# Expert rows loaded transposed, in place of a transpose on TensorE and a copy on VectorE

## What is computed

```python
# layer 1
z = layernorm(x)
agg = (adj > 0) @ z / max(degree, 1)
x = x + relu(concat(z @ W_self + b_self, agg @ W_nb + b_nb) @ W_comb + b_comb)
# layer 2: E = 8 experts, the best 2 of them for each row
xf = layernorm(x)
logits = xf @ Wg + bg
topk_scores, topk_idx = top_k(logits, 2)
topk_w = softmax(topk_scores)
h = gelu(einsum('nd,edh->neh', xf, W1) + b1)       # D = H = 256
y = einsum('neh,ehf->nef', h, W2) + b2
x = x + sum(topk_w * y[the two experts of the row])
```

## Time and profile before

| | |
|---|---|
| median of 3 runs | 551.37 us (549.81 to 551.41) |
| the profiled execution's own time | 551.93 us |
| its span | 550.1 us |
| PE busy | 439.9 us, 80% |
| DVE busy | 391.1 us, 71% |
| ACT busy | 272.6 us, 50% |
| POOL busy | 288.2 us, 52% |
| HBM read and written | 96.52 MB and 26.93 MB |

### The profile page before, as it was taken

The page is one execution under the profiler, slowest core; times in us unless marked ns, Lnnn a source line. Parts: engine busy times, 40 slices in busy tenths (PEclk is TensorE's granted clock), DMA queues, the critical chain, the costliest instruction groups (busy, mean ns, idle before and its releaser), DMA issues.

```text
span 550.1 us, 13137 instructions
## 1 busy us (share of the span) xinstructions
PE 439.9 (80%) x4321; PEld 382.9 (70%) x4321; DVE 391.1 (71%) x1197; ACT 272.6 (50%) x435; POOL 288.2 (52%) x305
## 2 busy tenths in 40 slices
PE   0015999999999999999999999635599999997730
PEld 0014889899898989898988898524378888786520
DVE  5717855686588888878857887574677777679871
ACT  3675452364255353654434444322367777776530
POOL 3993223234156575756564752646545556564570
PEclk9999999999999999999999999955989999999975
DMA  9975999999989999999996944512555555588565
GB/s 248 251 238 119 270 291 298 272 256 269 240 252 250 284 271 308 268 296 271 270 285 184 282 141 139 183 39 98 185 182 163 161 157 156 156 291 342 184 203 153
DMA packets 46785, 122.49 MB, mean 223 GB/s; under 512 B 8953, under 2 KB 18045, under 8 KB 45568
## 3 DMA queue, kind: packets, MB, share of 16 engines
q1 hardware_dynamic: 28896, 68.02, 47.4%
q0 software_dynamic: 16080, 50.49, 28.5%
q10 hardware_dynamic: 1744, 3.15, 2.1%
HBM read 96.52 MB, written 26.93 MB: 224 GB/s over the span
## 4 chain that ended last, share of the span: by engine, by line
PE 33%; DVE 15%; issue 15%; DMA 14%; POOL 13%; ACT 6%; SPq 1%; DVEq 1%; ACTq 1%; another core or an unknown queue 1%; POOLq 0%
PE bank L1224 8%; PE bank L1239 7%; PE bank L1115 5%; PE bank L1116 5%; DMA stage<-in_adj_dram,gidx 5%; POOL dispatched L545 4%; POOL stage L534 4%; DMA wst<-in_L_ffn_W_dram 4%; PE bank L1124 3%; PE bank L1211 2%; DMA stage<-in_adj_dram 2%; POOL z_lo L560 2%; DVE mask L769 2%; DMA x_sb<-in_x_dram 1%; DVE maskT L776 1%
## 5 line engine op out<-in xcount | busy, mean ns | idle before, releaser
L1115 PE MATMUL bank<-z_flat,maskT 128*128 128x257 f16 x1024 | 226.7, 273 | 0.0
L1116 PE MATMUL bank<-z_lo,maskT 128*128 128x256 f16 x1024 | 226.7, 273 | 0.0
L595 POOL DMA_INDIRECT pair_out<-rows,enum x78 | 80.9, 1038 | 64.8 <-DVE gate L1055 34.2
L534 POOL DMA_INDIRECT stage<-in_adj_dram,gidx x64 | 66.2, 1034 | 86.4 <-PE bank L1124 41.6
L1115 PEld LDWEIGHTS bank<-z_flat,maskT 128*128 128x128 fp8e4 x1024 | 100.2, 98 | 12.2
L1116 PEld LDWEIGHTS bank<-z_lo,maskT 128*128 128x128 fp8e4 x1024 | 100.2, 98 | 11.5
L545 POOL DMA_INDIRECT dispatched<-rows,slot x64 | 70.3, 1098 | 26.5 <-issue 19.2
L648 ACT ACTIVATE rows<-bank,rdeg 128x256 f16<-128x256 f32 x32 | 15.1, 473 | 134.3 <-DVE rdeg L829 110.7
L622 ACT ACTIVATE mask<-stage,m 128x2048 fp8e4<-128x2048 int32 x32 | 64.4, 2013 | 20.0 <-DMA stage<-in_adj_dram,gidx 17.9
L1224 PE MATMUL bank<-stage,w 128*128 128x256 f16 x468 | 61.3, 284 | 12.8 <-DVE stage L1028 11.0
L1239 PE MATMUL bank<-w,stage 128*128 x468 | 60.5, 278 | 9.9 <-DVE stage L1042 5.7
(11 more groups left out here) (175 smaller groups left out, 636.5 us busy)
## 6 DMA issues: line engine op xcount, KB each, us to landing
stage<-in_adj_dram SPq DMA_DIRECT2D x128, 256.0 KB
stage<-dispatched SPq DMA_DIRECT2D x39, 260.0 KB
wst<-in_L_ffn_W_dram SPq DMA_DIRECT2D x16, 256.0 KB
z_lo<-pair_out SPq DMA_DIRECT2D x4, 1024.0 KB
maskT<-pair_out SPq DMA_DIRECT2D x4, 1024.0 KB
out_dram<-x_sb SPq DMA_DIRECT2D x32, 128.0 KB
dispatched<-pad SPq DMA_DIRECT2D x15, 260.0 KB
x_sb<-in_x_dram SPq DMA_DIRECT2D x6, 256.0 KB, 9.1
```

Of the source, the lines that this page charges most:

```text
L534: gp.indirect_dma_start(out=stage[:, s, b - 2, :], out_offset=None, in_=adj_q[:, :], in_offset=bass.IndirectOffsetOnAxis(ap=gidx[:, 0:1], ...
L595: gp.indirect_dma_start(out=yp_dram[:, :], out_offset=bass.IndirectOffsetOnAxis(ap=enum[:, a, s:s + 1], axis=0), in_=ysb[:, a, s, :], in_o ...
L1115: mm(acc[u % 2][:, 0:D + 1], a, z_hi[:, i, :], start=(i == 0), stop=False)
L1116: last = mm(acc[u % 2][:, 0:D], a, z_lo[:, i, :], start=False, stop=(i == NT - 1))
```

## The change

The load of a tile's rows becomes two. The first takes the 512 float16 values of each of the 256 rows and transposes them on the way (`dma_start_transpose`): in SBUF each of 128 partitions then has, for each of four groups of 128 values, one run of 256 row entries, which is what the hidden product reads. The second takes the last four words of each row, 16 bytes, into a small buffer `meta`, with a semaphore of its own. PE's eight transposes and VectorE's copy to `exT` go, and `exT` with them. SP waits for the hidden product of tile t - 8 where it waited for its transposes. PE waits in front of the hidden product for the transposed load, and for the Gelu of two tiles before, whose banks it writes again. VectorE waits for the second load in front of the three small operations. PE now does only the (empty) step 0 ahead of the last rank matmuls, so that the hidden product of tile 0 comes behind them. Row s * 128 + p of a tile is now in place (p, s), where it was row 2p + s.

```diff
-        erow = cut(2 * R * RW).bitcast(F16).rearrange("p (a s n) -> p a s n", a=R, s=2)
-        erow32 = ring[:, 0:2 * R * RW].bitcast(I32).rearrange("p (a s n) -> p a s n", a=R, s=2)
-        erow_f = ring[:, 0:2 * R * RW].rearrange("p (a s n) -> p a s n", a=R, s=2)
+        xrow = cut(R * 2 * TT).bitcast(F16).rearrange("p (a q n) -> p a q n", a=R, q=2 * KT)
+        meta = cut(R * 2 * (RW - D)).rearrange("p (a s n) -> p a s n", a=R, s=2)
+        meta32 = meta.bitcast(I32)
...
-        exT = cut(2 * TT * KT).bitcast(F16).rearrange("p (a q n) -> p a (q n)", a=2, q=4)
...
-        LAST_RANKS, EARLY_PE, EARLY_DVE = NT + PR - B, 2, 1
+        LAST_RANKS, EARLY_PE, EARLY_DVE = NT + PR - B, 1, 1
...
                 if t >= R:
-                    sp.wait_ge(s_etp, t - R + 1)
+                    sp.wait_ge(s_ehp, 2 * (t - R) + 2)
                     sp.wait_ge(s_idc, t - R + 1)
...
-                sp.dma_start(erow_f[:, a], xs_dram[bass.ds(row, TT), :].rearrange("(p s) n -> p s n", s=2)).then_inc(s_er[a], 16)
+                sp.dma_start_transpose(xrow[:, a], xs_dram[bass.ds(row, TT), 0:D].bitcast(F16)).then_inc(s_er[a], 16)
+                sp.dma_start(meta[:, a], xs_dram[bass.ds(row, TT), D:RW].rearrange("(s p) n -> p s n", s=2)).then_inc(s_em[a], 16)
...
-                if live(known, 0, ET):
-                    dve.wait_ge(s_etp, t + 1)
-                    if known is None or known >= 2:
-                        dve.wait_ge(s_ehp, 2 * t - 2)
-                    v.tensor_copy(exT[:, u % 2, :], etp16[u % 2]).then_inc(s_exT, 1)
...
+                    dve.wait_ge(s_em[b], 16 * (j // R + 1))
                     apart(dve)
-                    v.scalar_tensor_tensor(gate2[:, r, :], erow32[:, b, :, EXP0], texp[:, at(j)], erow_f[:, b, :, DW],
+                    v.scalar_tensor_tensor(gate2[:, r, :], meta32[:, b, :, EXP0 - D], texp[:, at(j)], meta[:, b, :, DW - D],
...
-                if known == EARLY_PE:
+                if known == 2:
                     pe.wait_ge(s_slot, NG)
                 load_experts(pe, expert_of, (1, 2), t, u, known)
-                if live(known, 0, ET):
-                    a = u % R
-                    pe.wait_ge(s_er[a], 16 * (div(t, u, known, 0, R) + 1))
-
-                    for q in range(2 * KT):
-                        for s in range(2):
-                            last = nc.tensor.transpose(etp16[u % 2][:, q * TT + s * P:q * TT + s * P + P],
-                                                       erow[:, a, s, q * P:q * P + P], ident[:, :])
-                    last.then_inc(s_etp, 1)
                 if live(known, 1, ET):
                     j, r = t - 1, (u - 1) % 2
-                    pe.wait_ge(s_exT, j + 1)
-
+                    a = j % R
+                    pe.wait_ge(s_er[a], 16 * (j // R + 1))
+                    if j >= 2:
+                        pe.wait_ge(s_eg, 2 * j - 2)
...
-                                last = mm(hps[2 * r + h][:, 0:TT], w, exT[:, r, (xp * KT + kt) * TT:(xp * KT + kt + 1) * TT],
+                                last = mm(hps[2 * r + h][:, 0:TT], w, xrow[:, a, xp * KT + kt, :],
                                           start=(n == 0), stop=(n == 3 * KT - 1))
```

More of the change, by code:

```diff
@@ L250, in gnn_moe_kernel @@
         runi = cut_late(EB).bitcast(I32)
-        etp16 = [b_[:, :].bitcast(F16) for b_ in tps]
+        atp16 = [b_[:, :].bitcast(F16) for b_ in tps]
         mask32 = [mask[:, i].rearrange("p b j -> p (b j)").bitcast(U32).rearrange("p (b k w) -> p b k w", b=G, k=NG) for i in range(2)]
@@ L287, in gnn_moe_kernel @@
         s_er = [sem(f"expert_rows_loaded{i}") for i in range(R)]
-        s_etp, s_idc, s_exT, s_ehp, s_eg, s_ehi, s_elo, s_eyp, s_ey = (sem(n) for n in (
-            "e_transposed", "e_numbers_copied", "e_transposed_copied", "e_hidden_product", "e_hidden", "e_hidden_hi", "e_hidden_lo",
+        s_em = [sem(f"expert_row_ends_loaded{i}") for i in range(R)]
+        s_idc, s_ehp, s_eg, s_ehi, s_elo, s_eyp, s_ey = (sem(n) for n in (
+            "e_numbers_copied", "e_hidden_product", "e_hidden", "e_hidden_hi", "e_hidden_lo",
             "e_out_product", "e_out"))
@@ L653, in main_step @@
                     apart(act)
-                    sc.copy(aT[:, :], etp16[0]).then_inc(s_aev, 1)
+                    sc.copy(aT[:, :], atp16[0]).then_inc(s_aev, 1)
                 if live(known, LOGIT):
@@ L1048, in expert_step @@
                         dve.wait_ge(s_ysc[a], 32 * (j // RY))
+                    dve.wait_ge(s_em[b], 16 * (j // R + 1))
                     apart(dve)
-                    v.scalar_tensor_tensor(gate2[:, r, :], erow32[:, b, :, EXP0], texp[:, at(j)], erow_f[:, b, :, DW],
+                    v.scalar_tensor_tensor(gate2[:, r, :], meta32[:, b, :, EXP0 - D], texp[:, at(j)], meta[:, b, :, DW - D],
                                            ALU.not_equal, ALU.mult).then_inc(s_g2, 1)
-                    v.scalar_tensor_tensor(enum[:, a, :], erow32[:, b, :, EXP0], texp[:, at(j)], erow32[:, b, :, TOK],
+                    v.scalar_tensor_tensor(enum[:, a, :], meta32[:, b, :, EXP0 - D], texp[:, at(j)], meta32[:, b, :, TOK - D],
                                            ALU.not_equal, ALU.add)
                     dve.wait_ge(s_g2, j + 1)
-                    v.tensor_tensor(gate[:, a, :], gate2[:, r, :], erow_f[:, b, :, W0], ALU.add).then_inc(s_idc, 1)
+                    v.tensor_tensor(gate[:, a, :], gate2[:, r, :], meta[:, b, :, W0 - D], ALU.add).then_inc(s_idc, 1)
                 if known in (1, 2, 3, 4):
@@ L1158, in main_step @@
                     for q in range(2 * KT):
-                        nc.tensor.transpose(etp16[0][:, q * P:q * P + P], row16[:, at(j), q * P:q * P + P].rearrange("p o d -> p (o d)"), ident[:, :])
+                        nc.tensor.transpose(atp16[0][:, q * P:q * P + P], row16[:, at(j), q * P:q * P + P].rearrange("p o d -> p (o d)"), ident[:, :])
                     for q in range(2 * KT):
                         z = (z_hi, z_lo)[q // KT][:, at(j), q % KT * P:q % KT * P + P].rearrange("p o d -> p (o d)")
-                        last = nc.tensor.transpose(etp16[0][:, (2 * KT + q) * P:(2 * KT + q) * P + P], z, ident[:, :])
+                        last = nc.tensor.transpose(atp16[0][:, (2 * KT + q) * P:(2 * KT + q) * P + P], z, ident[:, :])
                     last.then_inc(s_atp, 1)
```

## The result

The changed kernel took 575.32 us (median of five runs, 573.76 to 578.93), the kernel before 549.81 beside it (548.90 to 551.41): a ratio of 1.048, 95% interval 1.045 to 1.052. It is slower by 25.5 us where 535 us, faster, was forecast, and it lies above the range's upper end of 563. The profiled execution has a span of 577.1 us.

The account below looks back on a forecast made before the run. PE's work and a two-step chain through PE and the Gelu were taken to bound the expert stage, 3.35 us a step. 551.93 - 12.2 - 3.0 - 1.0 = 535.7, so median 535 us; range 527 to 563.

Parts of the forecast that it names:

- the ring: Expert stage: output product, transposes, hidden product, Gelu, next output product; 6.66 us for two steps, 3.33 each.
- middle term: Delay from a hidden product's start to its Gelu: 1.99 us, put down to PE's full queue; might fall to 1.16.
- Part 1: PE's transposes go from the expert stage: step 2.90 us (2.68 to 3.11), gain 12.2 us over 27 steps.
- rival C: Gelu's delay isn't from PE's queue and grows by what the transposes leave: 545 to 549 us; chance 0.10.
- Part 2: VectorE's copy goes: gain in the six combine steps, 3.0 us taken, 3.6 at most, 1.5 at least.
- The combine steps: Six steps from tile 32's to tile 38's product, all DVE's work: 5.00 us each before, 4.4 forecast.
- Part 3: Start of the expert stage, 366 to 404 us, without five of VectorE's copies: gain 1.0 us, ends 0 and 3.
- Part 4: Transposing and small loads plus scatters: 2.1 us of DMA engines a tile, hidden in a 2.90 us step; cost nothing.
- The check that I had given: Sign against the forecast in the expert stage: loads pass each other at over 2.9 us.
- rival A: Transposing load handled piece by piece becomes the bound: 4.3 us a tile, 563 us; chance 0.17 for 551 to 600, 0.06 more.
- Rival B: Crowded DMA engines starve PE of instructions, splitting its matmul groups: up to 16 us lost, 551 us; chance 0.07.

Follow-up runs that it names:

- kind A: Not a changed kernel: the three of six chips (or occasions) on which the kernel before took 547 to 550 us.
- kind B: Not a changed kernel: the three of six chips (or occasions) on which the kernel before took 534 to 536 us.

## Why the prediction was wrong

**The bound and the ring.** PE's busy time and the ring of two steps were read rightly, and the two numbers that agreed (3.35 and 3.33) were both true. The step that failed is the sentence on the ring's middle term: "at 1.99 PE's signals come late behind a full queue of work". It was a guess on a row whose cause stood beside it, in the two scatters of the same timeline of the kernel before.

```profile
436.64 0.98 POOL L595 DMA_INDIRECT pair_out<-rows,enum  x1 [1.02 <-DVE gate L1055]
...
437.93 0.98 POOL L595 DMA_INDIRECT pair_out<-rows,enum  x1 [0.30 <-issue]
```

The second ends at 438.91; the signal of the product's first half, due at 438.63, is on record at 439.59, 0.7 us behind the scatter, and the Gelu starts at 439.80. I counted GpSimd by its busy time alone, 1.97 us a step, and so as an engine with room. The experiments without scatters and with four in a row show it to be a lock on PE's signals on kind A; a full queue leaves 1.05 us on kind B.

**Part 1.** The 0.44 us of the transposes left PE's order in both kinds. On kind B the step is 2.76, against 2.90 taken and 2.68 as the lower end, though from 3.07 and not from 3.35: 0.31 us a step of gain, 6.2 us over 20 steps. On kind A it went to 4.59, outside every end; the upper one, 3.11, supposed that the middle term could only stay or fall. It grew: over tiles 6 to 31 its median is 2.9 us (2.0 before), its longest 6.0. That a shorter step is what puts them in one row is argued from the rhythm of the timeline; that four in a row make such a loss is shown. This was the rival to write: rival C had the right term, but let it grow only by what the transposes leave.

**Part 2.** The combine steps were to be 4.4 us. On kind B there are six steps in 30.7 us behind tile 32 (468.12 to 498.81), 5.1 each with the stall in them and 3.6 behind it (four from 484.24 to 498.81). The kernel before takes 4.2 there (480.93 to 506.23), and 4.1 over the last four (489.91 to 506.23). So the copy's going was worth 0.4 us a step once the pairs were there, against 0.5 taken, and with the stall the six steps cost 5.4 us more in place of 3.0 less. The term had no place for a late load of pairs.

**Part 3** was too small: tile 5's product, just behind that stretch, came at 400.62 against 404.94 in the forecast's profile, and on kind B at 392.94 against 398.10, so 4 to 5 us earlier where 1.0 was taken and 3.0 was the upper end. How much of it is the first short steps can't be told apart.

**Part 4.** "Cost taken: nothing" failed. The terms: the two loads 1.94 us instead of 1.42, the scatters 0.85 instead of 0.65, SP's issue at least 2.7 instead of 1.6, since a transposing issue takes 1.25 us where the plain load in its place takes 0.38. The check that I had given, over 2.9 us between loads, is met at 2.96. But with one scatter left the two loads took 1.44 to 1.55, about what was priced: what failed is the sum, which added prices of half-empty engines as if packets did not wait for each other, and SP's issue. The direction was rival A's, the price not: 2.95 us for the transposing load alone was too high. With some 0.2 us off for the small load, an estimate from the plain-load kernel's 1.2 to 1.3 us for both beside 1.0 for the one load of the kernel before (kind B, q1's share of 48 us in each), the transposing load moves 256 KB in 1.7 us of full engines, about 150 GB/s, and in some 1.3 us, 200 GB/s, with one scatter left. The Trainium skill's 261 GB/s (page "DMA: Bandwidth & Descriptors", section "Latency and other measured facts") would make it an estimated 1.0; both measurements are slower.

**Rival B** didn't come: PE's groups on kind B are whole in the rows above. (In its own example the group took 4.68 us to its end, not 4.1.) **The chances**: slower had 0.24, all of it for causes in the transfers. None of it was for the cause that decided on kind A.

**Other chips.** On kind B, where the unaltered changed kernel ran on one of the three chips, the forecast's sign is right and its size wrong: 0.993, not 0.970. The 550 us of the earlier trace rows are 15 us longer than the same program on kind B: 6.8 us by tile 5's product, 7.5 from there to tile 32. In the first stage too 16 of 175 of PE's signals are late on kind A (40 to 366 us) and 0 of 181 on kind B; what each of these delays cost was not worked out.

No version here with right results beats both kernels on both kinds of chip.

## What to carry to other kernels

When a consumer starts late behind a producer that finished in time, look at what every other engine does in that gap, in both neighbouring steps, before putting it down to a queue; one engine's row of operations ending just ahead of the start is the hint. Then look at the semaphore's own record, if the trace has it: it tells a late signal from a late engine. Ask of each shortened step what it brings together that ran apart: an engine off the path can turn two small delays into one long one. And a load that does more work must be priced for its issue as well as its bytes, against the new, shorter step, and shares of engines don't simply add once they come near 1. Last, run both kernels on more than one chip before believing a gain of a few per cent.

## What the runs showed of the hardware that I had not expected

On some chips PE's completion signals are held while GpSimd's indirect transfers run one behind the other: 1.99 us from a product's start to its Gelu with two of them (1.05 without the effect), and 3.3 us of lateness with four. A lone scatter a step holds nothing that counts (2 late signals of 91, ACT's waits 0.5 us in all). Signals of VectorE and ScalarE are not held. On three of the six chips, and on the one of the first result, it was there; on three it was not, and the same program takes 535 us instead of 550. Why a chip is of one kind is open, as is the mechanism: the traces show that PE's signal is on record late, 0.6 to 1.1 us behind the last scatter, and not what holds it. A transposing load of 256 x 512 values of two bytes costs some 1.7 us of 16 engines in full queues and some 1.3 with one scatter less a tile (estimates, above), and 1.25 us of the issuing queue, where a plain one takes 0.38.
